# VectorE adds four more key tiles of a softmax attention into a second accumulator, and GpSimd's accumulator becomes single

## The reference

```python
q = (x @ Wq.T + bq).reshape(b, s, h, dh)
k = (x @ Wk.T + bk).reshape(b, s, h, dh)
v = (x @ Wv.T + bv).reshape(b, s, h, dh)
q = q * jnp.cos(rot)
k = k * jnp.sin(rot)
scores = jnp.einsum('bshd,bthd->bhst', q, k) / np.sqrt(dh).astype(np.float32)
scores = scores * spiral_weight[None, :, None, None]
attn = jax.nn.softmax(scores, axis=-1)
out = jnp.einsum('bhst,bthd->bshd', attn, v).reshape(b, s, d)
return out @ Wo.T + bo
```

## Time and profile before

| | us |
|---|---|
| median of 3 runs | 5951.64 |
| lowest and highest | 5946.49 to 5953.91 |
| the profiled execution's own time | 5950.2 |
| its span | 5948.2 |
| TensorE busy over the span | 5051.6 (85%) |
| VectorE busy | 2334.4 (39%) |
| ScalarE busy | 1822.7 (31%) |
| GpSimd busy | 1525.2 (26%) |

### The profile page before, as it was taken

How to read it: one execution, slowest core, us unless ns; L and a number is a source line. 1 busy time by engine, 2 the same in 40 slices (tenths; PEclk the granted TensorE clock), 3 DMA queues, 4 the chain that set the end, 5 groups by cost and what they waited for, 6 DMA issues and landing times. The chain is left out here.

```text
span 5948.2 us, 67863 instructions
## 1 busy us (share of the span) xinstructions
PE 5051.6 (85%) x25328; PEld 2536.2 (43%) x25328; DVE 2334.4 (39%) x3377; ACT 1822.7 (31%) x3499; POOL 1525.2 (26%) x951
## 2 busy tenths in 40 slices
PE   6037897799999999859999499999999979689997
PEld 3013343333333332356555245445445444455654
DVE  1853678357666667441221212222222220331111
ACT  2412554211555457421111133333333320121111
POOL 0011000102776772114545201111111110034444
PEclk9568999899999999969999799999999969789998
DMA  1000000000000000037888300000000012348887
GB/s 44 0 18 12 11 0 0 30 0 1 1 1 1 1 1 1 34 125 204 219 220 225 67 20 25 25 21 25 25 23 23 20 68 71 135 128 224 221 225 161
DMA packets 227748, 395.20 MB, mean 66 GB/s; under 512 B 31712, under 2 KB 119776, under 8 KB 226912
## 3 DMA queue, kind: packets, MB, share of 16 engines
q1 hardware_dynamic: 170144, 249.14, 12.6%
q0 software_dynamic: 57344, 142.64, 11.8%
HBM read 288.88 MB, written 107.02 MB: 67 GB/s over the span
## 5 line engine op out<-in xcount | busy, mean ns | idle before, releaser
L2173 PE MATMUL linb_pr_ps<-lin_z,linb_wt 128*128 128x512 f32 x2048 | 944.5, 606 | 9.0 <-ACT linb_wt L2257 9.0
L1365 ACT ACTIVATE attc_prob<-attc_ps 128x512 f32<-128x512 f32 x1024 | 548.9, 597 | 443.2 <-PE attc_ps L1276 442.4
L1239 POOL TENSOR_TENSOR attc_acc<-attc_acc,attc_prob 128x2048 f32<-128x2048 f32 x120 | 547.9, 4566 | 121.6 <-ACT attc_prob L1365 109.3
L1389 DVE TENSOR_REDUCE attc_peak<-attc_ps 128x2 f32<-128x1024 f32 x384 | 469.6, 1225 | 257.9 <-PE attc_ps L1284 257.9
L2173 PEld LDWEIGHTS linb_pr_ps<-lin_z,linb_wt 128*128 128x128 f32 x2048 | 380.6, 196 | 398.6 <-issue 388.7
L1276 PE MATMUL attc_ps<-att_q,att_k 32*128 32x512 f32 x2048 | 528.7, 616 | 0.0
L2347 DVE SCALAR_TENSOR_TENSOR linb_state<-linb_state,linb_sdec,linb_kv_ps 64x64 f32<-64x64 f32 x448 | 125.3, 280 | 859.0 <-PE linb_kv_ps L2212 851.8
L1284 PE MATMUL attc_ps<-att_k,att_q 32*128 32x512 f32 x1536 | 449.9, 663 | 0.0
L2147 POOL TENSOR_TENSOR linb_sq<-linb_osb 128x512 f32<-128x512 f32 x64 | 67.5, 1055 | 1295.1 <-ACT linb_osb L2279 1295.1
L2262 ACT ACTIVATE linb_proj<-linb_pr_ps 128x512 f32<-128x512 f32 x256 | 152.8, 597 | 625.5 <-PE linb_pr_ps L2173 625.4
L1297 PE MATMUL attc_ps<-attc_prob,att_v 128*32 128x256 f32 (+1 forms) x3472 | 316.5, 437 | 0.3 <-ACT attc_prob L1365 0.3
(11 more groups left out here) (516 smaller groups left out, 7766.7 us busy)
## 6 DMA issues: line engine op xcount, KB each, us to landing
moe1w_wgu<-in_L_ffn_gate_up_proj SPq DMA_DIRECT2D x32, 1536.0 KB, 12.4
moe2w_wgu<-in_L_ffn_gate_up_proj SPq DMA_DIRECT2D x32, 1536.0 KB, 12.4
moe1w_wd<-in_L_ffn_down_proj SPq DMA_DIRECT2D x32, 512.0 KB, 13.6
gated_features<-linb_gated SPq DMA_DIRECT2D x64, 256.0 KB, 2.1
linc_gt<-gated_features SPq DMA_DIRECT2D x8, 2048.0 KB, 8.3
moe2w_wd<-in_L_ffn_down_proj SPq DMA_DIRECT2D x32, 512.0 KB, 13.3
linb_wr<-in_L_attn_b_qkv_w SPq DMA_DIRECT2D x96, 128.0 KB, 2.6
residual_rows<-residual SPq DMA_DIRECT2D x2, 4096.0 KB, 12.9
```

Source lines behind the costliest of these rows:

```text
L1239: pool.tensor_tensor(acc[:, n % 2, :, :], before, prob[:, U % NP, :, :], ALU.add).then_inc(pool_done, 2 if at == 1 else 1)
L1365: nc.scalar.activation(prob[:, U % NP, h, :], ps[:, n % 3 if at < 0 else at % 6, :], ACT.Exp).then_inc(exp_done, 1)
L1389: V.tensor_reduce(peak[:, w // TT % 2, i % QH, 2 * hp:2 * hp + 2, b], ps[:, bank:bank + 2, :], axis=AX.X, op=ALU.max).then_inc(mx_used, 1)
L2173: last = nc.tensor.matmul(pr_ps[:, use % 2, :], wt[:, kind, k, :], z[:, k, t * NB:(t + 1) * NB], start=(k == 0), stop=(k == DT - 1))
```

## The change

VectorE now adds tiles 7, 8, 14 and 15 of a block into a new tile `late`, with three additions of 128x2048 (function `add_late`): tiles 7 and 8 after unit 8 is done, 14 before the reduces of unit 15, 15 before those of unit 16. In the first 12 blocks the use Z is gone on TensorE and VectorE, and F has two sources, `late` and `acc`, instead of three. The reciprocal reads F's PSUM bank, so the addition of `zsum` is gone there too, and the bank is given back when the reciprocal is done. `acc` is single: GpSimd's first addition of a block waits for F of the block before. The last four blocks still sum Z and F as before, with the single `acc`.

```diff
-        acc = L.sb("acc", [P, 2, QH, NB])
+        acc = L.sb("acc", [P, QH, NB])
+        late = L.sb("late", [P, QH, NB])
...
-                if done == SUMMED[1]:
+                if done == SUMMED[1] and U - LAG >= (DT - 1) * UNITS:
                     got.append("Z")
...
+        def late_after(U):
+            return len(SUMMED) * (U // TT) + max(2, SUMMED.index(U % TT) + 1)
...
-                    if at == 1 and n >= 2:
-                        pool.wait_ge(z_done, 2 * (n - 1))
+                    if at == 1 and n >= 1:
+                        pool.wait_ge(z_done, sums_before(n))
...
-                sources = [prob[:, (n - 1) % NP, :, :], prob[:, n % NP, :, :]]
+                if n < LAST_GROUP:
+                    pe.wait_ge(late_done, len(SUMMED) * (n // TT + 1))
+                    sources = [late[:, :, :]]
+                else:
+                    sources = [prob[:, (n - 1) % NP, :, :], prob[:, n % NP, :, :]]
...
-                    if (U - NP) % TT in SUMMED:
+                    if (U - NP) % TT in SUMMED and U - NP < LAST_GROUP:
+                        act.wait_ge(late_done, late_after(U - NP))
+                    elif (U - NP) % TT in SUMMED:
                         act.wait_ge(z_done, sums_after(U - NP))
...
+                if n < GROUPED:
+                    V.reciprocal(tot[:, :], ps[:, bank, :]).then_inc(mx_used, 1)
+                    dve.wait_ge(mx_used, use_at[U, "F"] + 1)
...
+            def add_late(U):
+                n, at = U // TT, SUMMED.index(U % TT)
+                dve.wait_ge(exp_done, (U + 1) * QH)
+                if at == 1 and n >= 1:
+                    dve.wait_ge(z_done, sums_before(n))
+                elif at > 1:
+                    dve.wait_ge(late_done, late_after(U) - 1)
+                before = prob[:, (U - 1) % NP, :, :] if at == 1 else late[:, :, :]
+                V.tensor_tensor(late[:, :, :], before, prob[:, U % NP, :, :], ALU.add).then_inc(late_done, 2 if at == 1 else 1)
...
+                if 1 <= U <= LAST_GROUP and (U - 1) % TT in SUMMED[1:]:
+                    add_late(U - 1)
```

More of the change, by code:

```diff
@@ L1180, in attention_heads @@
         vector_done = L.sem("vector_done")
+        late_done = L.sem("late_done")
         block = L.block()
@@ L1212, in rows_block, with sums_before @@
             return (f * TC + w // TT - 1) if w > TT else (f * TC - 1)
+        GROUPED = (DT - 1) * TC
+        def sums_before(n):
+            return n + max(0, n - GROUPED)
         def sums_after(U):
             n, i = U // TT, U % TT
-            return 2 * n + (1 if i in SUMMED[:2] else 2)
+            return sums_before(n) + (1 if i in SUMMED[:2] else 2)
+        def late_after(U):
+            return len(SUMMED) * (U // TT) + max(2, SUMMED.index(U % TT) + 1)
         def summed_by(U):
@@ L1233, in _ @@
                     pool.wait_ge(exp_done, (U + 1) * QH)
-                    if at == 1 and n >= 2:
-                        pool.wait_ge(z_done, 2 * (n - 1))
+                    if at == 1 and n >= 1:
+                        pool.wait_ge(z_done, sums_before(n))
                     if at >= 2:
                         pool.wait_ge(pool_done, n * len(POOLED) + at)
-                    before = prob[:, (U - 1) % NP, :, :] if at == 1 else acc[:, n % 2, :, :]
-                    pool.tensor_tensor(acc[:, n % 2, :, :], before, prob[:, U % NP, :, :], ALU.add).then_inc(pool_done, 2 if at == 1 else 1)
+                    before = prob[:, (U - 1) % NP, :, :] if at == 1 else acc[:, :, :]
+                    pool.tensor_tensor(acc[:, :, :], before, prob[:, U % NP, :, :], ALU.add).then_inc(pool_done, 2 if at == 1 else 1)
         @block.tensor
@@ L1308, in sums @@
                     pe.wait_ge(sem, count)
-                    sources.append(acc[:, n // TT % 2, :, :])
+                    sources.append(acc[:, :, :])
                 for at, src in enumerate(sources):
@@ L1411, in sums_out @@
                 if kind == "Z":
-                    dve.wait_ge(z_done, 2 * n + 1)
+                    dve.wait_ge(z_done, sums_before(n) + 1)
                     V.tensor_copy(zsum[:, :], ps[:, bank, :]).then_inc(mx_used, 1)
                     return
-                dve.wait_ge(z_done, 2 * n + 2)
-                dve.wait_ge(mx_used, use_at[U, "F"])
-                V.tensor_tensor(tot[:, :], ps[:, bank, :], zsum[:, :], ALU.add).then_inc(mx_used, 1)
-                dve.wait_ge(mx_used, use_at[U, "F"] + 1)
-                V.reciprocal(tot[:, :], tot[:, :]).then_inc(sum_step, 1)
-                dve.wait_ge(sum_step, n + 1)
+                dve.wait_ge(z_done, sums_before(n + 1))
+                if n < GROUPED:
+                    V.reciprocal(tot[:, :], ps[:, bank, :]).then_inc(mx_used, 1)
+                    dve.wait_ge(mx_used, use_at[U, "F"] + 1)
+                else:
+                    dve.wait_ge(mx_used, use_at[U, "F"])
+                    V.tensor_tensor(tot[:, :], ps[:, bank, :], zsum[:, :], ALU.add).then_inc(mx_used, 1)
+                    dve.wait_ge(mx_used, use_at[U, "F"] + 1)
+                    V.reciprocal(tot[:, :], tot[:, :]).then_inc(sum_step, 1)
+                    dve.wait_ge(sum_step, n - GROUPED + 1)
                 dve.wait_ge(o_out, n + 1)
@@ L1428, in add @@
                 if at == 1:
-                    dve.wait_ge(z_done, 2 * (n - 1))
+                    dve.wait_ge(z_done, sums_before(n))
                 else:
                     dve.wait_ge(vector_done, summed_by(U)[1] - 1)
-                before = prob[:, (U - 1) % NP, :, :] if at == 1 else acc[:, n % 2, :, :]
-                V.tensor_tensor(acc[:, n % 2, :, :], before, prob[:, U % NP, :, :], ALU.add).then_inc(vector_done, 2 if at == 1 else 1)
+                before = prob[:, (U - 1) % NP, :, :] if at == 1 else acc[:, :, :]
+                V.tensor_tensor(acc[:, :, :], before, prob[:, U % NP, :, :], ALU.add).then_inc(vector_done, 2 if at == 1 else 1)
+            def add_late(U):
+                n, at = U // TT, SUMMED.index(U % TT)
+                dve.wait_ge(exp_done, (U + 1) * QH)
+                if at == 1 and n >= 1:
+                    dve.wait_ge(z_done, sums_before(n))
+                elif at > 1:
+                    dve.wait_ge(late_done, late_after(U) - 1)
+                before = prob[:, (U - 1) % NP, :, :] if at == 1 else late[:, :, :]
+                V.tensor_tensor(late[:, :, :], before, prob[:, U % NP, :, :], ALU.add).then_inc(late_done, 2 if at == 1 else 1)
             z_before, zs = {}, 0
```

## The result

| | before | after |
|---|---|---|
| median of 4 runs, us | 5952.77 | 6017.56 |
| lowest and highest | 5946.49 to 5955.22 | 5996.67 to 6024.82 |
| span of the profiled execution | 5948.2 | 5994.9 |

The change makes the kernel 1.1% slower: the ratio is 1.0105, with a 95% interval of 1.0078 to 1.0131. So the first profile is of one of the shorter executions.

What follows compares the result with a forecast made beforehand. TensorE was taken to bound the attention's first 12 blocks. Four steps of +4.27 us a block (+51) plus 12 for the clock gave 63 us on 5950, with run medians 1.4 higher: forecast 6015 us, range 5965 to 6050.

Steps and rivals of the forecast that it cites:

- TensorE bounds the stage and VectorE's free time is in small grains: First 12 attention blocks: TensorE busy 795.87 of 826 us; VectorE idle only 0.59 and 0.72 us between reduces.
- the slack of 1.19: Bank wait in the attention: a VectorE reduce may be 1.19 us late before TensorE stands waiting.
- The sums: TensorE's sum products: Z and one source of F go, saving 2.58 us a block, all on the path.
- The addition after unit 8: VectorE's addition of tiles 7 and 8 delays the next reduce; TensorE gets its bank for A of unit 10 0.58 us late.
- The addition of tile 14: Before unit 15's reduces, VectorE's addition waits fully for GpSimd's last one; TensorE gets A16's bank 4.01 us late.
- The wait at A17: After tile 15's addition the reduce of A16 ends late, so A17's maxima start 1.81 us late.
- After F: End of block: zsum addition gone, but multiplication held by GpSimd's first addition; R starts later, +0.45 us a block.
- The four steps together: Sum for one of the 12 blocks, sums saved against new delays: +4.27 us, +51 us for 12.
- The clock: New TensorE waits before A16 make the clock fall: 0 to 2.8 us a block, taken as 1, 12 in all.
- no collision: Rival, chance 12%: VectorE's addition runs beside GpSimd's, a block costs 0.0 us, time 5952 us.
- The saving is kept: Rival, chance 6%: VectorE's lateness does not reach TensorE; 36 us saved, 5916 us.
- The clock falls twice in every block: Rival, chance 15%: adds 1.8 us a block to the main case, up to 22 us; 6037 to 6050 us.

Runs made afterwards that it cites:

- e12_place12: The changed kernel with twelve one-column memsets on VectorE ahead of layer 7, which nothing reads: 5994.84 us, ratio 1.0075 to the kernel before.
- e7_adds_only: The kernel before plus the change's three VectorE additions a block, result unused; Z, F and the double accumulator stay: 6007.24 us, ratio 1.0090.
- e1_reduce14: The change with tile 14's addition replaced by a one-operand maximum over 128x2048 numbers, TensorE summing tile 14 in F: 5966.73 us, ratio 1.0025 to before.
- e11_fill: The change with unit 16's two score products made three times ahead of the real ones in each block: 5997.25 us, ratio 1.0081 to before.
- e5_double_acc: The change with GpSimd's accumulator double again, so its first addition does not wait for F: 6012.53 us, ratio 1.0093 to before.
- v4_split_later: The change with tiles 7, 8, 14 added in halves, GpSimd's last addition postponed, tile 15 direct in F, double accumulator, maxima split moved later: 5913.31 us, ratio 0.9934.
- e4_single_acc: The kernel before with only GpSimd's accumulator made single, with its wait for F: 5957.42 us, ratio 1.0003.
- v2_two_halves: The change with only tiles 7 and 8 added by VectorE, in halves, tiles 14 and 15 direct in F, double accumulator: 5925.50 us, ratio 0.9955 to before.

## Why the prediction was right, and where it was not

The forecast was 6015 us; it is 6018. The direction and the main mechanism hold. The closeness owes something to luck: of the 63 us that I had put on the attention 39 to 46 arose there, and layer 7, of which I had said nothing, filled most of the gap. In `e12_place12`, where layer 7 is not lengthened, the same attention gives 5995.

- **TensorE bounds the stage and VectorE's free time is in small grains.** Right. `e7_adds_only` shows 62.6 us of cost in an attention in which VectorE had a third of its time free; halves of 1.22 us, 0.50 to 0.63 over the gaps and so within the slack of 1.19, cost nothing that can be seen.
- **The sums, -2.58 us a block.** The products went as worked out: from the values product at 1736.36 to the next round at 1738.65 F takes 2.29 - 0.57 = 1.72. What the stage gets back, net of the longer hold that comes with it, is 17 to 23 us for 12 blocks by `e7_adds_only`; the forecast had this hold in the next step but one.
- **The addition after unit 8, +0.58.** Too high. The addition is 2.28 as forecast, but in the block shown the next four rounds take 7.58 us where four undisturbed ones take 7.50, and the next seven 13.21 us, no more than undisturbed ones: the lateness was caught up at once.
- **The addition of tile 14, +4.01.** Right in mechanism and size: 6.26 us, ending 2.15 after GpSimd (forecast 2.14), with waits up to 4.3. The full wait was the right end of the range, though GpSimd's instruction is nearly three times as long as the one in the earlier trace rows. The Trainium skill, page "SBUF — State Buffer", section "Who interferes with whom", has the engine that issues first keep the shared ports for its whole instruction; the 6.26 us agree, and so do the 2.28 us of the maximum with one operand in `e1_reduce14`.
- **The wait at A17, +1.81.** In the change it is not there: TensorE waits once a block for the maxima, not twice. At 1.2 GHz the rounds A16 and B16 take so long that VectorE is ready first, and from the maxima of A16 to those of A17 it takes 1733.31 - 1727.28 = 6.03 us instead of 3.75, by the clock alone. Where the clock stays up, in `e11_fill`, the wait shows: the maxima of A17 start at 1729.58, and by the forecast's walk they are due at 1726.03 + 1.94 + 0.08 = 1728.05, so +1.53. Wait and slow clock overlap instead of adding up.
- **After F, +0.45.** Right in the number: R at 6.47 us in the shortest case (forecast 6.46), the multiplication at 1.80 (forecast 1.7). The reason is only half right. In `e5_double_acc`, where the multiplication is free, R still comes at 6.49 us on average (5.47 at the shortest). TensorE had waited for the reciprocal's bank, and the values product behind that wait runs at the lower level of the clock, 1.94 us instead of 1.06; it ends about when the held multiplication lets the reduce end.
- **The four steps together, +4.27.** From split to split of the maxima the shortest block takes 71.31 us after and 67.61 before: +3.70, with some of the clock in it. Three blocks of `e11_fill` without a slow stretch take 71.03, which makes +3.42 without the clock, or a little less if the repeated products cost something themselves. The 0.85 less than forecast are the 0.58 after unit 8 and the 0.28 at A17.
- **The clock, +1.** This is the term that failed. The mean block is 69.54 us before, 1.93 over the shortest, in which the clock stays up. In the change it is 72.26 and 72.84, which is 1.2 and 1.8 over the 71.03. So the clock's cost did not grow by 1 us a block; it fell by 0.1 to 0.7. The slow stretches did rise from 9 to 24, and by `e11_fill` those behind the new wait cost 0.9 to 1.5 us a block. But the kernel before had already paid for its own, in the 5950 that I added to, and in the change they lie in another place. Before, a slow stretch starts 0.3 to 2.0 us after R in 9 of 11 blocks and slows the rounds behind it; such a block takes 69.2 to 70.7 us instead of 67.6. In the change it starts 1.7 to 3.2 us before R, while reciprocal and held multiplication keep R back anyway: R comes 6.47 to 7.00 us after the start of the reciprocal, and 6.47 in `e11_fill`'s blocks with the clock up. The rows (columns as in the earlier trace rows, the granted clock is the third number from the end) of before, where R starts at 1728.74, and then of the change, where it starts at 1745.60:

```profile
1726.00:1729.00 3.00, 1.03 (x12) 0.24 (x4) 2.97 (x4) 0.78 (x2) 2.15 (x1) 1.00 0.00 0
1729.00:1735.00 6.00, 6.00 (x31) 2.08 (x28) 2.28 (x3) 1.08 (x2) 2.82 (x1) 0.50 0.01 4
```

```profile
1742.70:1746.00 3.30, 3.30 (x16) 0.55 (x12) 3.30 (x3) 0.20 (x1) 3.16 (x2) 0.50 0.00 0
1746.20:1750.00 3.80, 3.80 (x41) 1.32 (x42) 2.19 (x4) 1.77 (x4) 2.15 (x1) 1.00 0.02 6
```

  TensorE's wait for VectorE right before R, 21.7 us in 11 times before, is 0.5 us in 2 times in the change, from 1450 to 2230 us. I counted what the new waits cost the clock and not that the old falls would come to lie under waits. That this is the whole reason was not tried by itself.

Of the rivals, "no collision" falls by the 6.26 us. "The saving is kept" falls too, but its decisive point was right: with halves the lateness stays under the slack of 1.19 us, and `v4_split_later` at 5913 is where I had put that case (5916), by another route. "The clock falls twice in every block" came true in its condition (24 falls in 12 blocks) and not in its price, for the reason under the clock.

## What to carry to other kernels

Before giving work to an engine with "a third of its time free", compare the length of one new instruction with the gap between two of its old ones and with the slack of whoever waits for it, and ask what GpSimd does at that moment: here 2.28 us became 6.26, and two halves of 1.22 with GpSimd moved aside turned a loss of 1.1% into a gain of 0.66%. When a gain or loss is summed from a profile, cut the whole execution into stretches afterwards, untouched layers too, before believing that a forecast that fits was right for its reasons. And when waits move, ask where the clock's old falls come to lie: here they slid under a wait and cost less than before.

## What the runs showed of the hardware that I had not expected

- A cast of 128x16 numbers from SBUF to SBUF is held behind GpSimd for 3.33 us instead of 0.20, while a maximum over 128x2048 from one SBUF operand is not held at all (2.28 us beside the same chain). One operand alone is not what frees an instruction. The Trainium skill, page "SBUF — State Buffer", section "Who interferes with whom", counts copies and casts, which can enter the modes that use both ports of VectorE, among what can contend, and says that a `tensor_reduce` never does on this chip. The 3.33 and the 2.28 us agree; in which mode the cast ran, no run shows.
- Twelve instructions more or fewer on VectorE, far ahead of a loop in another layer, change that loop's six jumps by 0.9 to 3.7 us each and the kernel by some 23 us (6018 against 5995). A difference of 0.4% between two versions can be this alone: `e4_single_acc`, `v2_two_halves` and `v4_split_later` are compared with before among kernels with the short layer 7, while the change itself is not.
- Work that nobody needs can make a kernel faster: 2.85 us of repeated score products in each block kept the clock up (9 slow stretches instead of 23) and took 10 to 17 us off the attention (`e11_fill`).
